# Attention edge passes: all four weightings of a chunk stand together at the beginning of a stage in VectorE's order

## The reference, cut to what matters

```
k_j   = k[src] + e                                   # e = edge_attr @ We
alpha = einsum('ehc,ehc->eh', q[tgt], k_j) / sqrt(C)
amax  = segment_max(alpha, tgt)
ex    = exp(alpha - amax[tgt]);  denom = segment_sum(ex, tgt)
msg   = (v[src] + e) * (ex / denom[tgt])[..., None]
out   = segment_sum(msg, tgt)
```

## Time and profile before

| | |
|---|---|
| median of 3 timed runs | 9884.07 us (9882.16 to 9889.41) |
| span of the profiled execution, its own time | 12811.6 us |
| busy in it: POOL / VectorE / TensorE matmul / ScalarE | 6468.5 / 5537.1 / 5125.6 / 2975.8 us |

### The profile page before, as it was taken

How to read it: one execution, slowest core, us unless ns; L and a number is a source line. 1 busy time by engine, 2 the same in 40 slices (tenths; PEclk the granted TensorE clock), 3 DMA queues, 4 the chain that set the end, 5 groups by cost and what they waited for, 6 DMA issues and landing times. The chain is left out here.

```text
span 12811.6 us, 136822 instructions
## 1 busy us (share of the span) xinstructions
PE 5125.6 (40%) x24088; PEld 4316.2 (34%) x24088; DVE 5537.1 (43%) x17531; ACT 2975.8 (23%) x6690; POOL 6468.5 (50%) x6729
## 2 busy tenths in 40 slices
PE   0222222226222222222455554554544555445555
PEld 0222222224222222221344444444424444444443
DVE  3222222222222222226555555555555555555556
ACT  1000000002000000001344444444324444444443
POOL 3566566651655555550355555555315555555551
PEclk8555555558555555556666666666676666666666
DMA  3111111112111111112433333333243333333333
GB/s 91 41 43 42 42 43 43 43 41 73 43 42 42 41 41 42 42 42 88 128 115 113 111 112 108 120 110 115 85 143 111 111 111 114 106 113 117 114 114 100
DMA packets 625146, 1056.70 MB, mean 82 GB/s; under 512 B 265029, under 2 KB 422981, under 8 KB 598357
## 3 DMA queue, kind: packets, MB, share of 16 engines
q0 software_dynamic: 268320, 659.00, 18.0%
q1 hardware_dynamic: 263380, 326.66, 8.4%
q10 hardware_dynamic: 93408, 70.66, 1.7%
HBM read 978.20 MB, written 77.54 MB: 82 GB/s over the span
## 5 line engine op out<-in xcount | busy, mean ns | idle before, releaser
L1127 POOL DMA_INDIRECT conv_kv<-key_value,conv_src x3328 | 3217.8, 967 | 3544.9 <-DVE conv_pv L1186 1829.9
L537 POOL DMA_INDIRECT second_msg<-sage_hidden_projected,second_src x1664 | 1593.4, 958 | 1335.4 <-issue 758.1
L537 POOL DMA_INDIRECT first_msg<-sage_in,first_src x1664 | 1595.1, 959 | 1139.7 <-issue 587.6
L1383 PE MATMUL conv_ps_sums<-conv_pv,conv_sel 128*128 128x136 f32 x6656 | 1492.5, 384 | 319.7 <-issue 109.5
L584 PE MATMUL second_ps_sums<-second_msg,second_sel 128*128 128x129 f32 x3328 | 735.5, 400 | 1967.5 <-issue 945.4
L584 PE MATMUL first_ps_sums<-first_msg,first_sel 128*128 128x129 f32 x3328 | 740.5, 402 | 1940.3 <-issue 789.7
L1383 PEld LDWEIGHTS conv_ps_sums<-conv_pv,conv_sel 128*128 128x128 f32 x6656 | 1257.4, 270 | 501.6 <-issue 400.5
L1364 PE MATMUL conv_ps_query<-query_table,conv_selT 128*128 x6656 | 1320.8, 360 | 107.5 <-issue 107.2
L1151 DVE TENSOR_TENSOR conv_prod<-conv_ps_query,conv_kv 128x512 f32<-128x512 f32 x832 | 569.5, 685 | 1824.9 <-remote 1760.4
L584 PEld LDWEIGHTS second_ps_sums<-second_msg,second_sel 128*128 128x128 f32 x3328 | 663.3, 300 | 2040.0 <-issue 1882.4
L584 PEld LDWEIGHTS first_ps_sums<-first_msg,first_sel 128*128 128x128 f32 x3328 | 668.1, 302 | 2012.6 <-issue 1770.7
(11 more groups left out here) (209 smaller groups left out, 6412.2 us busy)
## 6 DMA issues: line engine op xcount, KB each, us to landing
conv_place<-place_rows SPq DMA_DIRECT2D x208, 1024.0 KB
conv_kv<-key_value,conv_src POOLq DMA_INDIRECT x3328
first_msg<-sage_in,first_src POOLq DMA_INDIRECT x1664
second_msg<-sage_hidden_projected,second_src POOLq DMA_INDIRECT x1664
key_value<-project_kv ACTq DMA_DIRECT2D x28, 896.0 KB
conv_pen<-run_penalties SPq DMA_DIRECT2D x832, 24.2 KB
project_hT<-conv_in_transposed SPq DMA_DIRECT2D x28, 448.0 KB
combine_hT<-conv_in_transposed SPq DMA_DIRECT2D x28, 448.0 KB
```

What stands on the lines that cost most here:

```text
L537: pool.indirect_dma_start(msg[:, slot, 0:D], None, table, bass.IndirectOffsetOnAxis(ap=src[:, h, k * GR + i:k * GR + i + 1], axis=0)).then ...
L1127: pool.indirect_dma_start(kv[:, h * CH + j, :], None, t.kv_d, bass.IndirectOffsetOnAxis(ap=src[:, h, j:j + 1], axis=0)).then_inc(gathered[ ...
L1383: last = pe.matmul(sums_of(step), sel[:, h * CH + step, :], pv[:, step, :, :].rearrange("p h w -> p (h w)"), start=True, stop=True)
```

## The change

All four weightings of chunk b are issued one after another at the stage's beginning; the two later places are gone. No instruction is added or removed, and no wait is changed. `weigh` itself is the same.

```diff
                     else:
                         c, h, g = a
                         if b is not None:
-                            weigh(b, 0)
-                            weigh(b, 1)
+                            for k in range(KG):
+                                weigh(b, k)
                     if b is not None:
                         dve.wait_ge(blk_in[b[1]], 16 * b[2] + 16)
...
                     m = mark(multiply(a, 2))
                     add(0, 3)
-                    if b is not None:
-                        weigh(b, 2)
                     add(1, 0)
                     need(m)
                     score_sum(a, 2)
...
                                       bc(rec[:, h, 2 * CH:3 * CH], 1, [P, HEADS, CH]), ALU.add).then_inc(scored, 1)
-                    if b is not None:
-                        weigh(b, 3)
-
                     dve.wait_ge(rows_ready, c + 1)
```

## The result

The kernel after takes 9800.3 us in the median (9796.9 to 9804.0, 4 runs) against 9886.4 (9882.2 to 9889.4) for the kernel before on the same chip: ratio 0.9915, 95% interval 0.9901 to 0.9929, 86 us faster. I had forecast no change.

The account below looks back on a forecast made before the run. POOL's pace of issuing gathers was taken to bound all four passes. The terms summed to 0 on the median of 9884 us, plus a few us for drain stages: forecast 9888 us, range 9850 to 9960, its own range 9870 to 9910.

Parts of the forecast that it names:

- The bound: All four gather passes of the timed runs go at the pace at which POOL issues gathers.
- The sum of 9866 us: Kernel before: POOL's gather busy time plus 0.30 us between gathers, attention 4216.2, GraphSAGE 4186.9, and 1462.5 us outside the passes.
- The 18 us: What the 9866 us lack to the median of 9884, taken as the worth of all other waits in the four passes.
- (1): Group 2's weighting moves to the stage's beginning; group 1's multiply, score sum and edge term come 1.2 us later, hidden, cost nothing.
- (2): Without group 3's weighting VectorE idles 0.58 us before the scan; no cost on the path, 121 us if cover is gone.
- (3): What hangs on `pv_ready` comes earlier, but POOL waits for it nowhere in the timed run: no gain, at most 18 us.
- W: Theory of the follow-up experiments: POOL had waited for group 3's weighting, which would explain the 86 us; no chance was given.
- I take 0.34, unchanged: Attention gathers held by VectorE's weightings lose 0.34 us a chunk before and after the change: 0 us, ends -71 and +141.
- The block's 0.24: GraphSAGE's loss in us a chunk from held gathers, where four such VectorE instructions stand in one block.
- Rival C: Faster: POOL's waits for group 3's weighting go (-18 us), holds fall to GraphSAGE's 0.24 (-21 us); 9845 together; chance 0.17.
- rival A: Slower: the block of four holds more gathers beside the stage's beginning; 62 us, 9946, at most 10025; chance 0.22.
- Rival B: Slower: VectorE bounds the timed run after all, so the filled wait costs up to 121 us, 10005; chance 0.07.

## Why the prediction was wrong, point by point

The bound: right. POOL's own pace bounds all four passes; it is busy for 66% of the span, and between gathers lie 0.3 us. The sum of 9866 us was near by luck in part: outside the passes of the kernel after lie 9802.2 - 2103.4 - 2103.1 - 2099.8 - 2102.3 = 1393.6 us instead of 1462.5, and attention took 4293 before the change instead of 4216. The 18 us that I took for "all other waits" hid some 77 us of attention, 64 of them gathers held longer than I had counted (3281.8 us busy for 3217.8).

(1), moves of group 2: hidden, as said. (2), the filled wait: right in size (109.2 us in 208 waits, 0.52 each, for 0.58), and right that it costs nothing on the first kind of chip (the run with 0.76 us more of VectorE took no longer). (3), no gain from waits: right; W fell.

The step that failed is the last one, "I take 0.34, unchanged". The mechanism was named; the sizes were wrong on one side. The Trainium skill (SBUF — State Buffer, "SBUF: two separate sides") has such an instruction block a GpSimd operation that reads SBUF for its whole length; the traces agree with that nearly, since the holds end 0.56 us after the beginning of an instruction recorded as 0.69 us. My reading that both gathers of the earlier trace rows "end their excess with the weighting" was off by the same 0.13 us: 6489.98 + 1.20 - 0.946 = 6490.23, where the weighting ends at 6490.37. What the runs showed in its place: on the first kind the kernel before pays (986 - 946) x 16 = 0.64 us a chunk, not 0.34; the kernel after pays (959 - 946) x 16 = 0.21, by the nearest row 0.24. So the term is (0.21 - 0.64) x 208 = -89 us. The 0.34 came from an execution in which POOL stood idle before the first and the last weighting of a stage (3.28 and 4.11 us). In its trace the pair held no gather in any stage, group 3's weighting 0.03 us a stage, and group 2's 0.32, nearly all of the 0.34. I had concluded that the timed runs have no such idle time and yet carried over a mean that depends on it. The block's 0.24 was there to read in GraphSAGE. For the split order an estimate from the window seen in the traces (0.5 us of the 1.25 between two gathers, a mean hold of 0.26 within it) gives 4 x 0.10 = 0.4 for four weightings beside a running POOL; even that is short of the 0.64, so the places against the gathers were unlucky as well.

Rival C, at 0.17, had the sign, but only 21 of the 89 us of this term, and another 18 us from waits that gave nothing; rival A had the mechanism with the wrong sign. Rival B, that VectorE bounds the passes and pays up to 121 us for the filled wait, isn't what the second kind of chip shows either: the loss there is 541 us, and VectorE's length, as said, costs nothing there. What the traces show between the kernel before and the one after is that POOL's wait for the weightings grows from 1829.9 us to 2431.8 and VectorE's before the scan from 509.1 to 1625.0 us, while the one before the multiply falls from 1760.4 to 1318.6. The waits of the kernel after there:

```profile
POOL conv_kv L1127 <- DVE conv_pv L1186: 2431.8, 204, 15.7
DVE conv_fwd L1267 <- remote: 1625.0, 195, 16.3
DVE conv_prod L1151 <- remote: 1318.6, 168, 18.8
```

What is late there are TensorE's results, once or twice a stage, by up to 18.8 us. TensorE's own waits in those places are put down to "issue", to nothing that the profile shows: 1563.5 us in 208 waits, up to 14.0 us, before it turns the scores in the kernel after, where the first kind has 584.9 us in 190 and at most 6.3. What makes them is open, and so is why the order of VectorE's instructions changes them. No run takes it apart.

## What to carry to other kernels

When the bounding engine is GpSimd issuing DMAs, look at the mean against the median of its instructions: here the excess was lost to VectorE instructions with two SBUF inputs, and an input in PSUM, or putting such instructions side by side, gave it back. That pays only where that engine's pace is the bound: on the second kind of chip, where the gathers waited for something else, both remedies cost time. Don't carry a mean duration from an execution in which the bounding engine idles to one in which it doesn't. And compare the span of a profile with the timed runs first: where they differ by 30%, ask on which chip it was taken before explaining it.

## What the runs showed that I had not expected

Two kinds of chips, 12820 and 9882 us for one kernel, a ratio of 1.30, with an order of instructions that gains 0.9% on one and loses 4.1% on the other. And a block of instructions with two SBUF inputs, one every 0.60 to 0.61 us, holds a stream of gathers of 1.25 us about once, whether it has two or six of them.
